# First attention layer: its weight preparation moved from a stage of its own into the attention's order of work

## The reference

```python
q = (hidden_states @ Wq).reshape(B, Sq, H, D)      # 256 -> 16 x 128
k = (encoder_hidden_states @ Wk).reshape(B, Skv, H, D)   # 128 -> 16 x 128
v = (encoder_hidden_states @ Wv).reshape(B, Skv, H, D)
q = rmsnorm(q, gq)
k = rmsnorm(k, gk)
scores = jnp.einsum('bqhd,bkhd->bhqk', q, k) * scale
attn = jax.nn.softmax(scores, axis=-1)
out = jnp.einsum('bhqk,bkhd->bqhd', attn, v)
...
x = x + jnp.tanh(g_xattn[0]) * _L0_xattn_ref(_layernorm(x, axis=-1), ctx_1024, ...)
```

## Time and profile before

| what | us |
|---|---|
| median of 3 runs (lowest to highest) | 1361.18 (1357.79 to 1362.24) |
| the profiled execution's own time | 1358.81 |
| its span in the profile | 1357.0 |
| start of the first scores (line 737) in the profile | 59.74 |
| start of the second quad's scores | 83.37 |
| last scores of this attention | 471 |

### The profile page before, as it was taken

The page is one execution under the profiler, slowest core; times in us unless marked ns, Lnnn a source line. Parts: engine busy times, 40 slices in busy tenths (PEclk is TensorE's granted clock), DMA queues, the critical chain, the costliest instruction groups (busy, mean ns, idle before and its releaser), DMA issues. The chain is left out here.

```text
span 1357.0 us, 23635 instructions
## 1 busy us (share of the span) xinstructions
PE 1271.7 (94%) x8163; PEld 1126.9 (83%) x8163; DVE 903.0 (67%) x2515; ACT 775.1 (57%) x2112; POOL 435.9 (32%) x420
## 2 busy tenths in 40 slices
PE   3799999999999969999999987999999999998998
PEld 3588888888888858888888875899898988887987
DVE  4688888888987657743433344667676677786867
ACT  3577777777777714322222255666666666545552
POOL 1365556654665523200000001222124242252430
PEclk8899999999999969999999998999999999999999
DMA  7000000000000400210000020000000003413435
GB/s 255 9 1 2 9 1 0 0 8 0 0 0 1 99 1 1 84 41 1 0 0 1 1 70 16 1 9 1 1 17 25 1 32 129 114 63 91 127 93 183
DMA packets 44237, 50.50 MB, mean 37 GB/s; under 512 B 14345, under 2 KB 36370, under 8 KB 43378
## 3 DMA queue, kind: packets, MB, share of 16 engines
q1 hardware_dynamic: 40354, 38.92, 9.7%
q0 software_dynamic: 3792, 10.40, 2.1%
HBM read 36.82 MB, written 12.49 MB: 36 GB/s over the span
## 5 line engine op out<-in xcount | busy, mean ns | idle before, releaser
L955 POOL TENSOR_TENSOR probs_a<-probs_a,rden_a 128x512 f32<-128x512 f32 x128 | 133.2, 1041 | 337.5 <-DVE rden_a L914 337.5
L98 PE MATMUL bank<-wvo_hi,pc_hi_a 128*128 128x256 f32 x512 | 154.0, 301 | 1.9 <-DVE pc_lo_a L921 1.9
L1321 ACT ACTIVATE act_g_f<-bank 128x512 f32<-128x512 f32 x64 | 38.2, 597 | 189.2 <-PE bank L100 189.2
L99 PE MATMUL bank<-wvo_lo,pc_hi_a 128*128 128x256 f32 x512 | 144.2, 282 | 0.0
L100 PE MATMUL bank<-wvo_hi,pc_lo_a 128*128 128x256 f32 x512 | 144.2, 282 | 0.0
L1378 DVE TENSOR_TENSOR hid_f<-act_g_f,bank 128x512 f32<-128x512 f32 x64 | 44.0, 688 | 143.3 <-ACT act_g_f L1321 143.3
L826 ACT ACTIVATE pc_hi_a<-bank 128x512 fp32r<-128x512 f32 x128 | 76.6, 598 | 107.3 <-PE bank L100 105.4
L917 DVE TENSOR_TENSOR pt_lo_a<-bank,pt_hi_a 128x512 fp32r<-128x512 f32 x128 | 87.8, 686 | 58.9 <-ACT pt_hi_a L823 58.3
L817 ACT ACTIVATE probs_a<-bank,nbias_a,q_r_a 128x128 f32<-128x128 f32 x256 | 114.4, 474 | 21.5 <-DVE nbias_a L908 21.5
L921 DVE TENSOR_TENSOR pc_lo_a<-bank,pc_hi_a 128x512 fp32r<-128x512 f32 x128 | 88.1, 688 | 45.3 <-ACT pc_hi_a L826 45.3
L98 PE MATMUL bank<-xt_hi_f,w_gu_hi_f 128*128 128x512 f32 (+1 forms) x256 | 102.0, 399 | 0.0
(11 more groups left out here) (304 smaller groups left out, 3989.9 us busy)
## 6 DMA issues: line engine op xcount, KB each, us to landing
xs_raw_f<-rows_in SPq DMA_DIRECT2D x39, 129.0 KB
q_raw_p<-in_L_xattn_Wq SPq DMA_DIRECT2D x4, 1024.0 KB, 8.5
y_tok_f<-rows_out SPq DMA_DIRECT2D x4, 1024.0 KB, 9.6
we_raw<-in_L_ffn_We_gate_up SPq DMA_DIRECT2D x2, 1408.0 KB, 10.8
o_raw_p<-in_L_xattn_Wo SPq DMA_DIRECT2D x1, 2048.0 KB, 10.2
x_sb<-in_x SPq DMA_DIRECT2D x4, 512.0 KB, 13.8
ctx_raw_a<-in_ctx SPq DMA_DIRECT2D x8, 256.0 KB, 2.8
o_early<-in_L_xattn_Wo SPq DMA_DIRECT2D x1, 2048.0 KB, 15.0
```

The lines of the kernel that those rows point to most:

```text
L98: nc.tensor.matmul(out, w[0], x[0], start=start, stop=False)
L99: nc.tensor.matmul(out, w[0], x[1], start=False, stop=False)
L955: nc.gpsimd.tensor_tensor(probs[:, i % 2, :, :], probs[:, i % 2, :, :], scale, ALU.mult).then_inc(sem("probs_scaled"), 1)
```

## The change

The block of the preparation goes for the first layer (the second layer keeps its own under the name `prepare_second`, with the same work as before). Its steps become words in the attention's list:
- WK0..3 and WQ0..3 split the 512 columns of Wk and Wq that one quad needs. Parts 0 and 1 (hi on ScalarE, lo on VectorE) stand ahead of the first scores; parts 2 stand in the first quad and parts 3 in the second (behind Rp2 and KH3), with lo on GpSimd.
- VT0..3 (four transpositions of Wv each, copied by ScalarE) and VO0..6 (products of two heads) stand ahead of the first scores, between the queries' steps; VO7 stands behind KTc3 of the first quad and its split VOc7 behind QTc3. VT and VO take their turn in the ring of two banks. The Tanh of the gates follows VOc7.
- SP now issues in this order: context of group 0, Wk part 0, tokens of group 0, Wq part 0, the two gains, Wk and Wq parts 1, Wv, Wo, parts 2 and 3, the other tokens, and the gates.
- Raw weights are loaded into the place of their own lo part (Wq, Wk, Wo) or of WVO's hi part (Wv and its transposition).
- The first group's four quads are written out as "first", and the loop runs over two groups instead of three.

The diff, cut to its core:

```diff
+    start = listed("""
+        WK0 CT0 CT1 LNA0 K0 Kc0 K1 Kc1 Kq0 LNB0 Kr0 K2 Kc2 Kq1 Kr1 K3 Kc3 Kq2 Kr2 WQ0 X0 X1 Kq3 Kr3 KN0 KH0 KH1 KH2 KH3 WK1 WQ1 VT0 VTc0 VT1 VTc1
+        VT2 VTc2 VT3 VTc3 Q0 Qv0 Qq0 Q1 Qv1 Qq1 VO0 Qr0 Qp0 VOc0 Q2 QT0 QTc0 VO1 Qv2 Qq2 VOc1 Qr1 Qp1 Q3 QT1 QTc1 VO2 Qv3 Qq3 VOc2 Qr2 Qp2
+        VO3 QT2 QTc2 VOc3 Qr3 Qp3 QT3 QTc3 VO4 KT0 KTc0 VOc4 VO5 KT1 KTc1 VOc5 KT2 KTc2 VO6 KT3 KTc3 VOc6""")
     start += [("S", 0, NQ), ("Sm", 0, NQ), ("CN", 0, pre)]
-    start += [s for s in quad_order(NQ) if s[0] not in ("W", "E")]
+    start += with_weights([s for s in quad_order(NQ) if s[0] not in ("W", "E")], {"KTc3": "VO7", "QTc3": "VOc7", "Rp2": "WK2", "KH3": "WQ2"})
     body = [s for j in range(1, NQ + 1) for s in quad_order(j)]
+    first = with_weights(quad_order(1), {"Rp2": "WK3", "KH3": "WQ3"})
+    first += [s for j in range(2, NQ + 1) for s in quad_order(j)]
...
-                with emit.engine.Fori(0, G - 1) as g:
+                for s in orders["first"]:
+                    emit("first", 0, *s)
+                with emit.engine.Fori(1, G - 1) as g:
...
+                keys_of(0)
+                tokens(0)
+                queries_of(0)
+                sp.dma_start(small[:, 4:5], a["L0_xattn_gq"].rearrange("(p a) -> p a", a=1)).then_inc(sem("gains_loaded"), 16)
+                sp.dma_start(small[:, 5:6], a["L0_xattn_gk"].rearrange("(p a) -> p a", a=1)).then_inc(sem("gains_loaded"), 16)
+                keys_of(1)
+                queries_of(1)
+                sp.dma_start(w["v_raw"][:, :], a["L0_xattn_Wv"]).then_inc(sem("wv_loaded"), 16)
+                sp.dma_start(w["o_raw"][:, :, :], a["L0_xattn_Wo"].rearrange("(h d) e -> d h e", d=P)).then_inc(sem("wo_loaded"), 16)
+                for t in range(2, NQ):
+                    keys_of(t)
+                    queries_of(t)
+                for m in range(1, G):
+                    tokens(m)
...
+                elif name == "VT":
+                    for a_ in range(4):
+                        last = nc.tensor.transpose(bank[:, a_ * P:(a_ + 1) * P], w["v_raw"][:, (4 * i + a_) * P:(4 * i + a_ + 1) * P], core.ident[:, :])
+                elif name == "VO":
+                    for h in (2 * i, 2 * i + 1):
+                        last = nc.tensor.matmul(bank[:, h % 2 * D:(h % 2 + 1) * D], w["v_t"][:, h, :], w["o_raw"][:, h, :], start=True, stop=True)
...
-                prepare_attention(nc, core, layer, a[f"L{layer}_xattn_Wq"], a[f"L{layer}_xattn_Wk"], a[f"L{layer}_xattn_Wv"],
-                                  a[f"L{layer}_xattn_Wo"], w, a, early, norm)
+                if layer == 1:
+                    prepare_second(nc, core, a["L1_xattn_Wq"], w, a, early, norm)
```

More of the change, by code:

```diff
@@ L212, in prepare_attention @@
         v_t = sb("v_t", [P, kv, P])
         loaded_q = [sem(f"loaded_q{k}") for k in range(KD)]
[L214 to L223, removed]
@@ L226, in prepare_attention @@
-        units = [("v_t", i) for i in range(nv_t)] + [("k_t", i) for i in range(nk_t)]
[L227 to L233, removed]
+        loaded_k, loaded_v, loaded_o = (early.loaded[n] for n in "kvo")
+        filled, hi_done, drained, split_done = (sem(n) for n in ("bank_filled", "hi_done", "transposes_drained", "split_done"))
@@ L254, in _ @@
                 for k in range(KD):
                     sp.dma_start(q_raw[:, k, :], Wq[k * P:(k + 1) * P]).then_inc(loaded_q[k], 16)
[L256 to L277, removed]
-            else:
-                @block.gpsimd
-                def _(pool):
-                    norm.root(pool, 0)
+                sp.dma_start(maskrow[:, :], a["mask_BxS2_bf1"].rearrange("b s -> (b s)").partition_broadcast(P)).then_inc(loaded_m, 16)
@@ L530, in orders_of, with with_weights @@
     last += [("LNF", 0, NQ)] + each(NQ, "W") + [("E", 0, NQ), ("E", 1, NQ)]
-    return {"start": start, "body": body, "last": last}
+    return {"start": start, "first": first, "body": body, "last": last}
+def with_weights(order, behind):
+    out = []
+    for name, i, j in order:
+        out.append((name, i, j))
+        for word in behind.get(f"{name}{i}", "").split():
+            out.append((word[:-1], int(word[-1]), 0))
+    return out
 def attention(nc, core, block, layer, w, a, gate_up, norm, norm_after, packed, router):
@@ L570, in attention @@
             ct = pair("ct", [P, GB, P])
+            small = sb("small", [P, 6])
             k_ss = sb("k_ss", [P, GB * QH])
@@ L602, in round_of @@
                 return g
+            if name in WEIGHTS:
+                return 0
             return quads(g, j)
-        per = {"X": 2, "CT": 2, "K": 4, "Q": 4, "KT": 4, "QT": 4, "NX": 2, "SR": 1, "RT": 1, "RK": 1, "XF": 2}
-        filled = {n: sem(f"{n.lower()}_filled") for n in per if n not in ROUTE and n != "XF"}
+        per = {"X": 2, "CT": 2, "K": 4, "Q": 4, "KT": 4, "QT": 4, "NX": 2, "SR": 1, "RT": 1, "RK": 1, "XF": 2, "VT": 4, "VO": 8}
+        filled = {n: sem(f"{n.lower()}_filled") for n in per if n not in ROUTE and n != "XF" and (L == 0 or n not in WEIGHTS)}
         released = {"X": sem("x_split"), "CT": sem("ct_split"), "K": sem("k_copied"), "KT": sem("kt_copied"),
@@ L616, in attention @@
                 rings[part] = ring, {s: (n + shift) % 2 for n, s in enumerate(ring)}
-            assert len(rings["body"][0]) % 2 == 0 and rings["start"][0][-2:] == rings["body"][0][-2:]
+            assert all(len(rings[part][0]) % 2 == 0 and rings[part][0][-2:] == rings["body"][0][-2:] for part in ("first", "body"))
         else:
@@ L676, in bank_free @@
                     return proj_bank[slots[step]]
-                before, gb = (ring, g) if at >= 2 else (rings["body"][0], g - 1)
+                if at >= 2:
+                    before, gb = ring, g
+                elif part == "first":
+                    before, gb = rings["start"][0], -1
+                else:
+                    before, gb = rings["body"][0], g - 1
                 n, i, j = before[at - 2]
@@ L882, in step @@
                 elif name == "KN":
+                    if part == "start":
+                        dve.wait_ge(sem("gains_loaded"), 32)
+                        nc.vector.scalar_tensor_tensor(out=w["gain"][:, :], in0=small[:, 4:5], scalar=float(P) ** 0.5, in1=small[:, 5:6],
+                                                       op0=ALU.mult, op1=ALU.mult).then_inc(sem("gain_made"), 1)
                     dve.wait_ge(sem("k_summed"), nth(4, m, GB - 1) + credit("k_summed"))
```

164 lines of the change are left out of this document (106 added, 58 removed).

## The result

The changed kernel takes **1349.95 us** (median of 5 runs, 1348.96 to 1351.24); the kernel before took 1358.39 on the same chip (5 runs, 1356.70 to 1362.24). The ratio is 0.9938, 95% interval 0.9923 to 0.9953: 8.4 us saved, between 6.4 and 10.5. Forecast were 1348.0, 1342.5 to 1354.5. The profiled execution took 1348.96 with a span of 1347.2, against 1358.81 and 1357.0: 9.8 us apart.

The account below looks back on a forecast made before the run. Nearly all of this attention's PE idle time lay in its first 59.7 us. A start 14.6 us earlier less 2.5 in the quads saves 12.1: 1346.7 or 1349.1 by reference, taken 1348.0, range 1342.5 to 1354.5.

Parts of the forecast that it names:

- first scores after 49: Sign of being wrong, at the attention's start: then look for PE steps of 0.43 us or a wait for Wo.
- the sum's two terms: First scores 14.6 us earlier at the start, less 2.5 us given back in the quads: 12.1 us saved.
- Q0 copied: Start: the first queries wait for the bank of Wv's third transposition group, 18.9, and are copied at 20.6.
- Loads: Rival: new loads at half speed land Wo at 31, not 17; about 3 us saved, 1356 to 1358; chance 0.04.
- Wk part 0 at 4.3: Head of the start: issued behind the context, Wk's first part lands at 4.3 us.
- The ring: Start's tail: two shared banks pace transpositions, queries and products, 3.7 us between the last products; first scores at 44.5.
- The lock: Start: DVE's split of WQ1 and GpSimd's power for KN exclude each other; first scores 44.5 or 45.7, taken 45.1.
- The quads: First two quads: VO7 and the added weight splits give back 1.8 and 0.7 us, together 2.5.
- covered, by 0.3 only: First quad: GpSimd's last Qp ends at 87.0, ahead of the bias that needs it at 87.3.
- The rival of exposed quads: ACT's 1.5 and GpSimd's 3.35 us exposed in both quads; 7 us saved, 1352 to 1354; chance 0.11.
- Low clock to the first scores: Rival: PE stays at 1.2 GHz through the start; 8 us on the path, 4 saved, 1355 to 1357; chance 0.09.
- Slower: Rival: PE enters the first quad at the lower clock and stays, some 20 us more; 1375; chance 0.03.

Follow-up runs that it names:

- filler's kernel: Changed kernel plus 24 never-read matmuls in PE's gaps ahead of the first scores, to hold the clock up; 1347.70 us, ratio 0.9923.
- the rearranged order: Changed kernel with products VO and Wv's transpositions on banks of their own, the transpositions put together first, WQ1's split behind the second queries; 1339.81 us, ratio 0.9863.
- e_quads: Changed kernel with the splits of Wk and Wq parts 2 and 3 moved from the quads to ahead of the first scores; 1350.62 us, ratio 0.9956.
- e_bankq: Changed kernel with products VO on the two output banks and the splits of parts 2 and 3 ahead of the first scores; 1340.30 us, ratio 0.9871.
- e_loop: e_bankq with the first group back in the loop over three groups instead of written out; 1340.47 us, ratio 0.9881.

## Why the prediction was right, and where it was not

The direction, the range and within 2 us the time held: 8.4 us saved where 12.1 were summed. "Put first, they start the chain as soon as they land" held, and PE's first key product is the proof: 7.31, where before even the context was used only at 33.42. But the prediction's own signs of being wrong speak against its start: "first scores after 49" is among them, and they came at 50.48, with PE at the lower clock in the tail. Of the other signs of being right, KN near 17 (18.41), products 3.7 us apart at the end (4.4 and 5.4) and second scores 25.4 behind the first (27.0) all missed; no product waited for a load, and the bias waited 0.51, under the 1 us named. So of the sum's two terms the large one was too large by 5.3 us, step by step:

| step of the prediction | forecast | measured | late |
|---|---|---|---|
| context used by PE | 3.6 | 3.86 | 0.3 |
| first key product (Wk landing) | 6.05 | 7.31 | 1.3 |
| KN0 | 17.0 | 18.41 | 1.4 |
| Q0 copied (transpositions of Wv at clock 0.50) | 20.6 | 22.52 | 1.9 |
| ring, Q0 copied to first scores | 23.9 | 27.96 | a further 4.1 |
| first scores | 44.5 to 45.7, taken 45.1 | 50.48 | 5.4 |

**Loads.** The first step that failed is "Wk part 0 at 4.3": worked out from the rate between two landings of long transfers and the 2.7 us of a transfer alone. The trace has 5.52. What lies behind it, the dense DVE chain to KN, went as followed in this profile: 11.1 us from the first product to KN0, forecast 10.95. That leans on the clock's rise at 10.97, in the middle of the keys; in the other kernels with this start it took 11.1 to 12.4.

**Q0.** VT started 1.3 late with KN, and its 16 transpositions took until 20.6 at the lower clock, 3.4 us, where 3.0 were forecast.

**The ring.** The largest miss: 4.1 us more than the 23.9 of the forecast, in two parts. With the clock at 1.00 the filler's kernel took 25.2 (first queries copied at 22.77, scores 47.99), 1.3 over. Its timeline shows where:

```profile
26.95 0.66 PE L729 MATMUL bank<-ident,q_tok_a 128*128 128x128 f32 x4 [0.37 <-DVE wvo_lo L905]
...
28.39 1.13 PE L693 MATMUL bank<-wo_raw,wvt_raw 128*128 128x256 f32 x4 [0.32 <-DVE q_tok_a L910]
...
41.47 1.13 PE L693 MATMUL bank<-wo_raw,wvt_raw 128*128 128x256 f32 x4 [0.60 <-DVE wvo_lo L905]
...
45.52 1.03 PE L693 MATMUL bank<-wo_raw,wvt_raw 128*128 128x256 f32 x4
```

QT0 to VO1 takes 1.44 (1.45 in the change: 26.73 to 28.18), forecast 0.6: VO1 goes into the bank of the third queries, whose copy on DVE I had let pass as done. It was not: in the start that copy (Qv2) waits until QT0 has read the place that it writes, and in the change it starts at 27.44, as QT0 ends. That is 0.8 of the 1.3. From there on the forecast's distances nearly hold: 13.1 from VO1 to VO5 (12.95 forecast), 4.05 from VO5 to VO6 (3.9). The other 2.8 is the clock: in the change VO5 to VO6 took 5.4. The forecast's danger of the lower clock stood in a rival, as all or nothing (8 us on the path if it lasts from 19 on), and no term of the sum asked whether PE, with such waits between its pieces, keeps the level there. It was a part of that, 2.8 here and 1.7 in the first quad. The price of a product on PE, 0.85, does not follow from the record count given for it (4 records at 7 per us are 0.6), but the change has 0.78 (28.18 to 28.96) and 0.94 (23.72 to 24.66), so that number did no harm.

**The lock.** The term between 44.5 and 45.7 came to nothing. In the changed kernel's timeline GpSimd's power for KN and DVE's split of WQ1, which reads two SBUF inputs, ran beside each other:

```profile
18.67 3.28 POOL L997 TENSOR_TENSOR k_r_a<-k_ss_a,half 128x16 f32<-128x16 f32 x1 [7.62 <-DVE k_ss_a L921]
```

```profile
19.10 1.24 DVE L898 TENSOR_TENSOR wq_lo<-wq_raw,wq_hi 128x1024 fp32r<-128x1024 f32 x1
```

The split took 1.24, as one that ran alone at 15.36 (1.23), and the power 3.28 instead of 2.90. The rule that I cited, the Trainium skill's SBUF — State Buffer, section "SBUF: two separate sides", has the two exclude each other for a whole instruction; by it one of them would have ended 1.2 or 3 later. This trace disagrees for an operation on 128x16, at most 0.4 us passed; in the rearranged order, where the split stands elsewhere, the same power takes 2.90. For the split of 128x2048 the rule did agree, and so it does for the bias of 128x4 that ended with GpSimd's split, above. Here the end of the range without loss was the nearer one, 0.6 better than taken.

**The quads.** 2.5 were forecast, 3.4 + 0.5 = 3.9 measured at the third scores. 1.7 of it is the low clock at the first quad's head: the fillers' kernel, with the clock up, had 25.34 and 27.08. Against before that is 1.7 + 0.5 = 2.2, so the term without the clock was right within 0.3. Half of what the first quad keeps over before with the clock up (25.34 against 23.63) is not the parts but VO7's turn in the ring: with the products on their own banks and the parts in place the quad takes 24.44, in three profiles, 0.8 over before. The lines named beforehand, in the changed kernel's DVE timeline at the head of the second and of the third quad:

```profile
79.97 0.68 DVE L931 TENSOR_REDUCE nmax_a<-bank 128x4 f32<-128x512 f32 x1
80.76 0.16 DVE L945 TENSOR_TENSOR nbias_a<-nmax_a,q_r_a 128x4 f32<-128x4 f32 x1
...
107.05 0.16 DVE L945 TENSOR_TENSOR nbias_a<-nmax_a,q_r_a 128x4 f32<-128x4 f32 x1 [0.51 <-POOL q_r_a L1014]
```

GpSimd's last power ahead of the first of them, and PE's first key product of the second quad:

```profile
79.54 1.01 POOL L1014 TENSOR_TENSOR q_r_a<-q_ss_a,half 128x4 f32<-128x4 f32 x1 [0.92 <-DVE q_ss_a L927]
```

```profile
78.72 0.50 PE L98 MATMUL bank<-wk_hi,ct_hi_a 128*128 128x512 f32 x1
```

In the first, the bias follows DVE's own reduction with no wait for GpSimd, whose last power ends at 80.55: "covered, by 0.3 only" held. In the second it waits 0.51 for GpSimd, forecast 0.6. But that wait cost nothing: it lies behind the third scores, and from the third to the fourth it is 27.25 us (104.57 to 131.82), against 27.35 before (109.95 to 137.30). The 0.48 by which the quad ahead of it is longer, forecast 0.7, come from elsewhere: K0 starts 1.21 behind the scores (77.51 to 78.72) instead of 0.91, for it takes the bank of VO7, which DVE has split at 78.66, and with the products on their own banks it is 0.91 again (63.55 to 64.46); the rest goes with the parts (e_quads). The size of that term was near by luck, its cause was not the one named. The rival of exposed quads gave 1352 to 1354 and so nearly the sum's true remainder, but by a mechanism that these lines speak against. Writing out the loop's first turn costs and gives nothing, as priced: 0.07 us a group in the profiles of the two kernels that differ in that alone, and 0.2 between their medians.

**What made up for it.** The sum at the last scores is 5.5 us, the runs say 8.4 (6.4 to 10.5) and the profiled pair 9.8. The pair gained 2.65 us from the last scores to the feed-forward's first tokens (27.3 before, 24.65 after) by a higher clock, and some 1.6 more behind. Filler at that end did not carry over into the medians, and the kernels with other loads, quads or banks showed 24.7 to 27.4 there, 24.7 in e_bankq and e_loop, whose medians are no better for it. The median time less the last scores lies between 882.6 and 887.4 us for all of them, in no order. So the 1 to 3 us between 5.5 and the runs stay unassigned: the scatter of one profile is as large. The prediction's number was nearer than its sum because it lay between two references and because this remainder had the fitting sign; that is luck, not method. (The ends of the range are each 0.3 us off their own terms: 16 from 1358.8 are 1342.8, 7 from 1361.2 are 1354.2. Nothing hangs on it.)

**The rivals.** Low clock to the first scores: real in part, about half its price (2.8 ahead of the scores and 1.7 behind them, of 8). Quads: its time, not its cause. Loads: Wk late by 1.2, Wo not by 14: its bytes were there by 23.7, when the first product ran, and no wait of PE for it is in the list. Slower: the clock rose in the first quad between 55 and 56, some 5 us after its start, so it cost 1.7 and not 20.

## What to carry to other kernels

Work that is put into idle gaps also takes its turns in whatever the neighbours share; here seven products in a ring of two banks cost each transposition a wait for two engines, and two idle banks gave back 11 us, the clock's share included, more than the whole change. Follow the banks with the clock beside them: a stretch in which PE, DVE and ACT are all idle for a good part is a turn-taking chain, and PE may lose its clock there and at the head of the next stage. Before a wait in a row is counted as a cost, look whether the next station comes later for it: one of 0.51 us here did not. And before crediting the rest of a saving to a place far from the edit, run the same code twice: 2 us between profiles were scatter here.

## What was not expected of the hardware

- The granted clock's column reads 1.00 for the first 16 us, although the first key products stepped at 0.43 us (8.30 to 8.73) and those from 10.97 on at 0.23: until the first rise the column does not tell the level, the steps do. In the kernel with Wv on its own banks it reads 1.00 up to 20 us while PE steps at the lower level. The Trainium skill, TensorE: Matmul & The Clock Gate, section "What's actually happening", calls the lower clock the default; the steps agree.
- The clock fell not only after an idle time: from 22 to 38 PE was busy 11.55 of 16 us in pieces, with no gap over 2 us, and was at 0.57 at 38 and 0.50 until 44. With 14.4 busy of 16 in the filler's kernel it stayed at 1.00.
- Two 256 KB loads issued 0.5 us apart are usable some 1.7 us (3.86 and 5.52) or 0.9 us (4.88 and 5.75) apart, where the rate of the 2 MB load gives about 0.7 us for 256 KB.
- A bias of 128x4 on DVE, 0.16 us elsewhere, took 1.32 and ended with a 2.40 us split on GpSimd that had begun 1.09 ahead of it.
- The same start in two executions had its first scores 1.5 (kernel before) and 2.1 us (changed kernel) apart. The steps differ in when the clock rose: in the changed kernel at 10.97 in one, and in the other not in the keys at all, which step at 0.43 until 13.79.
